# First attention's output projection: one f32 product becomes three passes over high and low halves

## The reference, cut to what matters

```python
x = x + jnp.tanh(g_xattn[0]) * _L0_xattn_ref(_layernorm(x, axis=-1), ctx_768, ...)
x = x + jnp.tanh(g_ffn[0]) * _L0_ffn_ref(_layernorm(x, axis=-1), ...)   # top 256 of 2048 tokens by router score
...
def _L0_xattn_ref(x, y, Wq, bq, Wkv, bkv, Wo, bo):
    q = (jnp.einsum('bld,ed->ble', x, Wq) + bq).reshape(b, l, h, dh)
    ...
    att = jax.nn.softmax(jnp.einsum('blhd,bmhd->blmh', q, k) * scale, axis=2)
    out = jnp.einsum('blmh,bmhd->blhd', att, v).reshape(b, l, d)
    return jnp.einsum('bld,ed->ble', out, Wo) + bo
```

## Time and profile before

| | us |
|---|---|
| median of 3 runs (1784.87 to 1787.61) | 1785.94 |
| the profiled execution's own time | 1783.94 |
| its span | 1782.2 |

### The profile page before, as it was taken

The page is one execution under the profiler, slowest core; times in us unless marked ns, Lnnn a source line. Parts: engine busy times, 40 slices in busy tenths (PEclk is TensorE's granted clock), DMA queues, the critical chain, the costliest instruction groups (busy, mean ns, idle before and its releaser), DMA issues. The chain is left out here.

```text
span 1782.2 us, 25660 instructions
## 1 busy us (share of the span) xinstructions
PE 1559.6 (88%) x9526; PEld 954.2 (54%) x9559; DVE 1276.9 (72%) x2066; ACT 887.7 (50%) x1431; POOL 575.7 (32%) x556
## 2 busy tenths in 40 slices
PE   6798888998678979968999999999997878888887
PEld 4444444443356648745666665666664534445543
DVE  5576777887542546654777775777766599999996
ACT  4455555554544426426334333443432477777773
POOL 3132343233310002113112021111200297777781
PEclk9899999998888889989999999999999899999998
DMA  4112221212622424531020101102011330121211
GB/s 168 42 48 96 95 71 48 72 72 95 251 92 96 185 87 142 200 112 48 1 83 25 60 35 51 60 25 83 1 60 36 120 124 30 66 68 67 79 54 48
DMA packets 73283, 142.34 MB, mean 80 GB/s; under 512 B 8417, under 2 KB 17781, under 8 KB 72906
## 3 DMA queue, kind: packets, MB, share of 16 engines
q1 hardware_dynamic: 71914, 137.55, 22.3%
q0 software_dynamic: 960, 3.15, 0.6%
q10 hardware_dynamic: 288, 0.00, 0.0%
HBM read 97.67 MB, written 43.01 MB: 79 GB/s over the span
## 5 line engine op out<-in xcount | busy, mean ns | idle before, releaser
L2899 POOL TENSOR_TENSOR E_y<-E_y,E_centre 128x1024 f32<-128x1024 f32 x64 | 151.2, 2363 | 6.9 <-ACT E_y L2928 3.6
L1454 ACT ACTIVATE D_oT<-D_OB 128x512 fp32r<-128x512 f32 x64 | 38.3, 599 | 222.3 <-DVE D_OB L1771 222.3
L2787 PE MATMUL E_HP<-E_xT,E_w1q 128*128 128x512 bf16 x482 | 127.2, 406 | 2.4 <-ACT E_xT L2905 0.4
L2891 POOL TENSOR_SCALAR E_centre<-E_hs,E_cw,E_cb 128x512 f32<-128x512 f32 x64 | 109.4, 1709 | 53.5 <-DVE E_hs L2987 53.4
L1743 DVE TENSOR_TENSOR D_q_low<-D_PJ,D_q_high 128x512 fp32r<-128x512 f32 x60 | 41.5, 692 | 95.4 <-ACT D_q_high L1430 95.4
L2812 PE MATMUL E_YT<-ident,E_y 128*128 128x128 f32 x496 | 69.0, 285 | 42.9 <-DVE E_am L3005 39.1
L2996 DVE SCALAR_TENSOR_TENSOR E_y<-E_hs,E_cw,E_y 128x512 f32<-128x512 f32 x128 | 105.6, 864 | 0.0
L2800 PE MATMUL E_OP<-E_w2q,E_yb 128*128 128x512 bf16 x446 | 103.3, 385 | 0.7 <-issue 0.7
L1523 PE MATMUL D_PJ<-D_xT_high,D_wq_high 128*128 128x512 f32 x240 | 100.7, 420 | 0.1
L588 PE MATMUL A_TX<-A_wo,A_oT 128*128 128x512 f32 x176 | 90.4, 639 | 7.1 <-PEq L1106 7.1
L1523 PE MATMUL D_PJ<-D_xT_high,D_wq_low 128*128 128x512 f32 x240 | 94.4, 393 | 0.0
(11 more groups left out here) (433 smaller groups left out, 4136.5 us busy)
## 6 DMA issues: line engine op xcount, KB each, us to landing
A_res<-in_x SPq DMA_DIRECT2D x8, 1024.0 KB, 5.4
xn_d<-A_xn SPq DMA_DIRECT2D x8, 1024.0 KB, 4.7
x_d<-A_res SPq DMA_DIRECT2D x8, 1024.0 KB, 6.1
W_raw<-in_w1T SPq DMA_DIRECT2D x16, 512.0 KB, 3.6
W_raw<-in_w2T SPq DMA_DIRECT2D x16, 512.0 KB, 3.8
...
```

The costliest lines, as they stand in the source:

```text
L2787: mm = pe.matmul(HP[:, i % 2, e, :], w1q[:, k, m * P:(m + 1) * P], XT[n % 2][:, k, :], start=k == 0, stop=k == KD - 1)
L2891: pool.tensor_scalar(U[i % 2][:, 0, :], hs[i % NBUF][:, 0, 1:TILE + 1], cw[:, 2 * p, 1:2], cb[:, 2 * p:2 * p + 1], ALU.mult, ALU.add).then ...
L2899: pool.tensor_tensor(y, y, U[i % 2][:, :, :], ALU.add).then_inc(t0, 1)
```

## The change

The output projection takes the attention's result and `Wo` in halves and does three passes for each k. `Wo`'s high half is a second ScalarE copy behind its scaling (`scale_wo`), its low half a GpSimd subtraction (`low_wo`), both in tile 0. The division now writes its result back into `OB`; ScalarE copies the high half from there (`high_o`) behind the turned maxima and the ranking's rows, and VectorE subtracts the low half (`low_o`) behind the addition. The router's score moves ahead of the addition. `weigh` of the next slot waits for the low half (`o_ok`), the sums of exponentials for the division (`o_div`). To make room, buffers share memory: k's full value lies over its low half, x's halves over the gathered rows (so the first gather waits for all queries), and `junk`, `later` become bf16.

```diff
@@ project_out
             if part == 0:
                 pe.wait_ge(o_ok, QT * (n + 1))
+            h, l = oh[n % 2], ol[n % 2]
             for k in range(part * QT // parts, (part + 1) * QT // parts):
-                mm = pe.matmul(out_bank(n, c), oT[n % 2][:, k, c * P:(c + 1) * P], wo[:, k, :],
-                               start=k == 0, stop=k == QT - 1)
+                for o, w in ((h, woh), (h, wol), (l, woh)):
+                    mm = pe.matmul(out_bank(n, c), o[:, k, c * P:(c + 1) * P], w[:, k, :],
+                                   start=k == 0 and o is h and w is woh, stop=k == QT - 1 and o is l)
@@ GpSimd, gather and the loop over slots
             pool.wait_ge(id_ok, 2 * (b + 1))
+            pool.wait_ge(q_mm, QT * STEPS)
...
+            def low_wo(k):
+                pool.wait_ge(wo_hi, k + 1)
+                pool.tensor_tensor(wol[:, k, :], wo[:, k, :], woh[:, k, :].bitcast(F32), ALU.subtract).then_inc(wo_ok, 1)
...
                 for c in range(SUB):
+                    if n == 0 and c:
+                        low_wo(c - 1)
...
+                    if n == 0 and c == SUB - 1:
+                        low_wo(c)
@@ ScalarE
-                need(act, o_ok, k - 1)
+                need(act, o_div, k - 1)
...
-                act.activation(wo[:, k, :], wo[:, k, :], ACT.Copy, scale=tg).then_inc(wo_ok, 1)
+                act.activation(wo[:, k, :], wo[:, k, :], ACT.Copy, scale=tg).then_inc(wo_sc, 1)
+                act.wait_ge(wo_sc, k + 1)
+                act.activation(woh[:, k, :], wo[:, k, :], ACT.Copy).then_inc(wo_hi, 1)
+
+            def high_o(s):
+                act.wait_ge(o_div, s + 1)
+                act.activation(oh[s // GROUPS % 2][:, s % GROUPS, :], OB[:, :], ACT.Copy).then_inc(o_hi, 1)
...
                 keep_sums(act, s)
+                high_o(s)
                 keep_found(act, s)
@@ TensorE, weigh and the loop
                 n, j = divmod(s, GROUPS)
+                need(pe, o_ok, s)
                 for g in range(HG):
...
-                need(pe, o_ok, s)
+                need(pe, o_div, s)
@@ VectorE
                 dve.wait_ge(pv, s + 1)
-                dve.tensor_tensor(oT[s // GROUPS % 2][:, s % GROUPS, :], OB[:, :], rz[:, :], ALU.mult).then_inc(o_ok, 1)
+                dve.tensor_tensor(OB[:, :], OB[:, :], rz[:, :], ALU.mult).then_inc(o_div, 1)
+
+            def low_o(s):
+
+                dve.wait_ge(o_hi, s + 1)
+                dve.tensor_tensor(ol[s // GROUPS % 2][:, s % GROUPS, :], OB[:, :],
+                                  oh[s // GROUPS % 2][:, s % GROUPS, :].bitcast(F32), ALU.subtract).then_inc(o_ok, 1)
...
                 divide(s)
+                score(dve, s)
                 add_out(dve, s)
-                score(dve, s)
+                low_o(s)
```

More of the change, by code:

```diff
@@ L158, in context_tensors @@
     sb = lambda n, s, d: ctx.enter_context(nc.sbuf_tensor(L["name"] + n, s, d))
-    kh, kl = (sb(n, [P, L["inner"] // P, NB, CTX], F32R) for n in ("k_high", "k_low"))
-    return kh, kl, sb("V", [P, NB, L["inner"]], F32)
+    shape = [P, L["inner"] // P, NB, CTX]
+    kh = sb("k_high", shape, F32R)
+    with ExitStack() as over:
+        kT = over.enter_context(nc.sbuf_tensor(L["name"] + "kT", shape, F32))
+    return kh, sb("k_low", shape, F32R), sb("V", [P, NB, L["inner"]], F32), kT
 class ContextStage:
@@ L342, in chosen_tensors @@
     sb = lambda n, s, d=F32: ctx.enter_context(nc.sbuf_tensor("S_" + n, s, d, side="right"))
-    return {"idx": sb("idx", [P, NB * HALVES], mybir.dt.uint32), "xs": sb("xs", [P, NB * HALVES, D]),
-            "base": sb("base", [P, NB * HALVES, D]), "got": ctx.enter_context(nc.semaphore("S_gathered"))}
+    with ExitStack() as over:
+        halves = [over.enter_context(nc.sbuf_tensor(f"A_xT_{n}", [P, KD, TILE], F32R, side="right")) for n in ("high", "low")]
+    return {"xs": sb("xs", [P, NB * HALVES, D]), "base": sb("base", [P, NB * HALVES, D]),
+            "idx": sb("idx", [P, NB * HALVES], mybir.dt.uint32), "xT_halves": halves,
+            "got": ctx.enter_context(nc.semaphore("S_gathered"))}
 def by_act(q):
@@ L381, in narrow_attention @@
         upto, less, ties = keep("upto", [P, NC]), keep("less", [P, CHUNKS]), keep("ties", [P, CHUNKS])
-        later, lost = keep("later", [P, NB, NC, NC]), keep("lost", [P, NC])
+        later, lost = keep("later", [P, NB, NC, NC], BF16), keep("lost", [P, NC])
         rank = keep("rank", [P, NC])
@@ L389, in narrow_attention @@
         X = sb("x", [P, SUB, D])
-        xt = [sb(f"xT{i}", [P, KD, P]) for i in range(2)]
-        xh, xl = sb("xT_high", [P, KD, TILE], F32R), sb("xT_low", [P, KD, TILE], F32R)
+        with ExitStack() as over:
+            xt = [over.enter_context(nc.sbuf_tensor(f"{name}xT{i}", [P, KD, P], F32, side="right")) for i in range(2)]
+        above = keep("above", [P, S], BF16)
+        xh, xl = chosen["xT_halves"]
         qh, ql = sb("q_high", [P, QT, TILE], F32R), sb("q_low", [P, QT, TILE], F32R)
-        oT = [sb("oT0", [P, QT, TILE]), oT_last]
-        wq = oT_last[:, :, :].rearrange("p q n -> p (q n)").rearrange("p (k n) -> p k n", k=KD)
+        oT = [sb("oT0", [P, 2, QT, TILE], F32R), oT_last]
+        oh, ol = [o[:, 0, :, :] for o in oT], [o[:, 1, :, :] for o in oT]
         pr = sb("probs", [P, HG, TILE])
@@ L437, in narrow_attention @@
         s_mm, s_ex = sem("s_made"), sem("probs_ready")
[L438 removed]
+        z_mm, pv, z_r, o_div, o_hi, o_ok = (sem(n) for n in (
+            "z_made", "pv_made", "rz_ready", "o_divided", "oT_high", "oT_ready"))
         z_ln, z_ex, z_t = sem("z_ln"), sem("rz_guess"), sem("z_times_guess")
@@ L714, in _ @@
                 sp.dma_start(X[:, c, :], x_dr[0, 0, :, c]).then_inc(first_in[c], 16)
-            sp.dma_start(wq, rows(io[L["wq"]])).then_inc(w_in, 16)
+            sp.dma_start(wq[:, :, :], rows(io[L["wq"]])).then_inc(w_in, 16)
             sp.dma_start(bq[:, :], io["bq0"]).then_inc(w_in, 16)
```

27 lines of the change are left out of this document (16 added, 11 removed).

## The result

The changed kernel took 1780.08 us (median of 16 runs, 1770.90 to 1785.65) against 1787.38 us for the kernel before (16 runs, 1779.69 to 1791.23): ratio 0.9967, 95% interval 0.9953 to 0.9981, so 7.3 us faster where 8 were forecast. The profiled execution took 1779.8 us, 4.1 less than before's. The whole time of one execution is a weak witness here: runs of one kernel spread over 15 us, so totals are read from the medians. Single slots are a good one: in the profiled execution of the second series each of the slots 0 to 29 came out within 0.12 us of the first, although its span is 5.1 us longer. So what follows reads single slots from the traces. The granted clock there is TensorE's, a share of its full one, as a mean over the stretch; over short stretches the traces show it at 1.00 or at 0.50, here called full and lower.

The account below looks back on a forecast made before the run. TensorE was taken to pace the plain slot, VectorE 1.07 us behind, with VectorE pacing other slots and a third chain at tile ends. Terms summed to -7.65, say -8 us, from median 1785.94 to 1778.0 us; range 1770 to 1787.

Parts of the forecast that it names:

- third slots: Slots 6, 10, 14, 18, 22, third of each tile: forecast at +0.3 us together.
- VectorE-paced slots: Slots where VectorE sets the pace: each changes by 0.72 us minus its idle before the addition; seven plain ones +1.4.
- tile ends: Slots 7, 11, 15, 19, 23: the first three shorten by 1.5, 1.2, 0.7 us, slots 15 and 19 lengthen by 0.1 each.
- the addition still waits: Sign to watch: VectorE without idle before the addition in slots 9 to 21.
- The first half is lost at the maxima, the second stays: TensorE-paced slots: only the second half's gain survives; slots 4, 8, 12 at -0.40 us each, slot 16 at -0.35.
- VectorE's 0.72 us a slot: VectorE's new subtraction takes 691 ns, 0.72 us a slot with issue.
- Slot 22: VectorE's 2.44 us wait for a lower-clock second half shrinks with the passes: -0.7 us.
- Slot 3: First tile end, no projection yet to shorten: pays for the new copy ahead of chunk 2, +0.9 us.
- The score's move: The router's score ahead of the addition fills VectorE's wait for the projection, 0.22 to 0.71 us in eleven slots.
- the whole gain: Rival: maxima don't hold TensorE and tile ends follow the projection; -20 to -24 us, 1764 us; chance 0.10.

Follow-up runs that it names:

- e7: The changed kernel unaltered, run again as a yardstick on a second chip: 1782.48 us, ratio 0.9969 to the kernel before.
- e5: The kernel before with one edit, the router's score moved ahead of the addition: 1779.41 us, ratio 0.9952.
- e3: The changed kernel with GpSimd's four bias additions all in a tile's last slot, behind its last low half of x: 1774.83 us, ratio 0.9935.
- e6: The changed kernel with ScalarE's new copy behind the copies of chunks 2 and 3 at every tile end: 1781.51 us, ratio 0.9969.
- e8: The changed kernel with GpSimd's bias additions late and, in slot 3 alone, ScalarE's new copy behind those of chunks 2 and 3: 1775.49 us, ratio 0.9943.
- e10: The changed kernel without ScalarE's copy and VectorE's subtraction, keeping three passes and the score ahead of the addition: 1764.75 us, ratio 0.9869.
- e1: The changed kernel with the three passes alone: no ScalarE copy or VectorE low half, score back behind the addition: 1778.56 us, ratio 0.9958.
- e4: The changed kernel with the router's score back behind the addition, ahead of the low half: 1798.59 us, ratio 1.0069.
- e2: The changed kernel with all added work, but one f32 product of the high halves instead of three passes: 1789.64 us, ratio 1.0015.

## Why the prediction was right, and where not

The sign and the size hold: 7.3 us against 8. The terms hold less well. The sum came out because errors cancelled, and that was luck: the third slots lost 6.6 us more than forecast, and the VectorE-paced slots (2.0 us better than forecast) and the tile ends (4.5, most of it clock) gave it back. The profiles show less than the medians: the first attention gained 4.6 and 4.4 us in the two executions, and the end of its slots near 460 us, up to which the sum's terms make -6.15, moved by -4.0 (460.70 to 456.67), in e7, whose slots began 3.1 us later, by -0.9. Two other things went against the forecast: the addition still waits (0.33 to 1.42 us in slots 10, 14, 18 and 22), and there is more time at the lower clock between 96 and 460 us (granted 0.93, was 0.94).

- *The first half is lost at the maxima, the second stays.* Right: 0.23 us of wait in slots 8 and 16 (forecast 0.3 to 0.4), slots 4, 8, 12 shorter by 0.31 to 0.32 (forecast 0.40), slot 16 by 0.35 as forecast.
- *VectorE's 0.72 us a slot.* The kind of term was right, the size not: the subtraction takes 0.60 from start to start (266.04 to 266.64), and the score's move saved more than the wait it fills (0.67 us in slot 17 of e5, wait 0.61). The seven plain VectorE-paced slots came out at -0.6, forecast +1.4.
- *The third slots.* The step that failed. The sum has +0.3, the runs show +6.9, of which e3 took back all. The prediction had the hint: VectorE's small subtraction, both operands in SBUF, took 1.28 us at 240.38, beside GpSimd's low halves of x, and 0.23 at 259.48. I carried that to the maxima alone. The new subtraction, with one operand in PSUM, was not held (681 ns in the mean, in the rows by line above). What I didn't ask is what else stands near a GpSimd operation: the comparison, both operands in SBUF, had missed it by 0.05 us. Caught by it, the comparison took 1.37 us instead of 0.35. Slot 22, forecast at -0.7, came out at +0.46, of which the stall is 1.02.
- *The tile ends.* The chain was near in sum (-4.2, forecast -3.2), less so one by one: slots 7, 11, 23 -3.2 (forecast -3.4), slots 15, 19 -1.0 (forecast +0.2). Another 3.5 us is clock (17.1 us of these slots at granted 0.50, was 27.3), which the forecast's sum leaves out.
- *Slot 3.* +3.0, forecast +0.9; the difference is ten of the twelve passes at granted 0.50. e6 and e8 moved the copy, and slot 3 was back at 13.06 us. The lower clock cost 2.1 us here (5.05 against 2.97 in e6), near the 2.33 that lie between slots 15 and 16 before (5.32 and 2.99); the sum has no term for it.
- *The score's move.* I priced it only as a filler of the idle time. Alone it gave 8.5 us, the passes alone 7.7, so neither is clearly the larger part of the change. In the prediction's own terms, eleven slots' waits (0.22 to 0.71 us, 5.5 in total) stood in the trace, and they could be had without the change. What each edit is worth hangs on the others: the score's place 8.5 us alone, about 15 on top of the passes (e10 against e1) and 18 in the changed kernel (e4); the passes 7.7 alone, about 14 on top of the score's place (e10 against e5) and 9 to 11 in the changed kernel (e2).
- *The rival "the whole gain".* It was given 0.10 and 20 to 24 us; e10, without the halves' own work, gave 22.5. That is the rival's size and not its mechanism: the maxima hold TensorE in e10 just the same (0.22 or 0.23 us in slots 4, 5, 9, 12 and 13), and much of its gain is the score's place. What keeps the change from it is the halves' own work: 15 to 17.5 us, against about 9 in my sum (eleven times 0.72, before the waits filled are taken off, and 0.9 in slot 3).

Not tried: a version without the copy but with the subtraction, which would part the cost of the halves' own work further.
